# Attention layer: the softmax shift as transposed split columns, and an accumulator copy and its first use in another order

## The chip, the cores and the metric

The kernel runs on one core of one Trainium2 chip. The metric is the device time of one execution in microseconds (us). A change of more than 0.2% in either direction counts as a difference here; less counts as none.

## What is computed

Two layers over an image batch of 4 x 64 x 64 positions with 256 channels. Layer 0 (a state-space and convolution block) is untouched. Layer 1 is self-attention over the 4096 positions of each image, cut here to what matters:

```
f = xf @ Wf + bf            # keys,    32 channels
g = xf @ Wg + bg            # queries, 32 channels
hh = xf @ Wh + bh           # values, 256 channels
scores = einsum("bnd,bmd->bnm", g, f)
attn = softmax(scores, axis=-1)
o = einsum("bnm,bmc->bnc", attn, hh) @ Wo + bo
out = gamma * o + xf
```

The softmax needs a shift for each query: the maximum of its scores over all 4096 keys, taken off before the exponential.

## The kernel before

Layer 0 takes the first 2.6 ms and leaves keys, queries, values (each value as a high and a low part) and the residual in DRAM. `layer1` then works through 32 chunks of 512 queries (8 chunks for each of 4 images). A chunk `c` has 32 steps `m`, one for each 128 keys. Each engine runs its own instruction stream with explicit semaphores; the order is written out by hand in the function `body` of each engine, and nothing reorders it. The functions named below are on the lines of the profile.

In a step TensorE issues:

- `scores` (L1392), one pass into `ps_s`, for step m+2: it runs two steps ahead (`AHEAD`), so the scores of the next chunk's steps 0 and 1 are made in steps 30 and 31. The softmax shift is folded into this matmul: rows 96 and 97 of the query tile `gq` hold the negated maximum as a high and a low part, and the key tile `f_st` holds 1.0 in these rows.
- `scores_max` (L1375), one or two passes into `ps_m`, in steps 0 to 25: the scores of the next chunk against all keys, only for their maximum.
- `values_high` (L1401), four passes into `ps_o[0]` and `ps_o[1]`: the high part of the probabilities, times both parts of the values; `values_low` (L1409), two passes for the step before: the low part.
- in step 28 `spread_max` (L1382), which brings the maxima of the next chunk from one per partition to one per column.
- in steps 2, 4 and 6 the end of the chunk before: `sum_keys` (L1416) and `turn_half` (L1430, transposes of the accumulator copy `o_ch`).

ScalarE writes `ph` (L1502) and `probs` (L1504) from the scores, and in step 2 (`take_sums`) copies the old `ps_o[0]` into `o_ch` (L1488) and the old key sums `ps_a` into `sums` (L1492). VectorE reduces each `ps_m` to a maximum (`reduce_max`, L1514), adds the probabilities up in `ps_a` (L1543), copies the old `ps_o[1]` at the head of a chunk (`take_o`, L1548), and makes the shift in `finish_max`: the row maximum (L1519) in step 26, four diagonal 128 x 128 tiles `diag` (L1523) in step 27, and in step 29 two passes over the spread result (L1528 and L1532) that write rows 96 to 127 of `gq`. GpSimd makes `pl`, the low part of the probabilities (L1296). The queue of SyncE loads the queries of chunk c+2 (L1319) once the last `scores` of chunk c has run; at the last chunks of an image it also loads keys and values for the next image.

The first `values_high` of a chunk overwrites `ps_o`, so it waits on `o_out`, which the two copies into `o_ch` raise. The first `scores` of a chunk waits on `max_ok` for the finished `gq`.

Of the kernel before, what the change touches and what calls it, by code (L numbers as in the profile page):

```python
# [19 lines left out]
P = 128  # L20
# [1156 lines left out]
for _r in range(KEYS):  # L1177
    MAX_AT.setdefault(_r * MAX_STEPS // KEYS, []).append(_r)
MAX_REDUCE, MAX_DIAGONAL, MAX_SPREAD, MAX_ROWS = MAX_STEPS, MAX_STEPS + 1, MAX_STEPS + 2, MAX_STEPS + 3
AHEAD = 2  # L1180
# [6 lines left out]
def layer1(nc, keep, f_d, g_d, v_d, xres_d, out):  # L1187
# [5 lines left out]
    with ctx:  # L1193
# [18 lines left out]
        part_max = sb("part_max", [P, QT, PER_IMAGE])  # L1212
        row_max = sb("row_max", [P, QT])
        diag = sb("diag", [P, QT, P])
        max_hi = sb("max_hi", [P, TOK], F32R)
        pick = sb("pick", [P, 1])
        res = sb("res", [P, 2, QT, C])
# [61 lines left out]
        def _(pool):  # L1279

            for i, (part, value) in enumerate((
                    (f_st[96:P, :, :].bitcast(F32), 0.0), (pick[96:P, :], -1.0), (f_st[96:98, :, :].bitcast(F32), 1.0),
                    (pick[96:97, :], 0.0))):
                if i:
                    pool.wait_ge(const_ok, i)
                nc.gpsimd.memset(part, value).then_inc(const_ok, 1)

# [76 lines left out]
        def _(pe):  # L1364
# [13 lines left out]
            def spread_max(c):  # L1378

                pe.wait_ge(max_ok, 4 * c + 2)  # L1380
                for qt in range(QT):
                    mm = pe.matmul(ps_m[0][:, qt * P:(qt + 1) * P], ones[:, :], diag[:, qt, :], start=True, stop=True)  # L1382
                mm.then_inc(bcast_ok, 1)
# [55 lines left out]
            def body(c, par, img, half, at):  # L1439
                for m in range(KEYS):  # L1440
                    ending = m == KEYS - 1
                    values_high(c, m, 0)
                    if at != "first":
# [5 lines left out]
                    if at != "last":  # L1449
                        for r in MAX_AT.get(m, []):  # L1450
                            scores_max(c + 1, 1 - par, half + par, r, img + 1 if at == "turn" else None)
                        if m == MAX_SPREAD:
                            spread_max(c + 1)
                    if not ending:
                        values_high(c, m, 1)
# [14 lines left out]
            spread_max(0)  # L1470
            pe.wait_ge(const_ok, 4)
            for m in range(AHEAD):
# [6 lines left out]
        def _(act):  # L1479
# [3 lines left out]

            def take_sums(c):

                act.wait_ge(lo_done[0], KEYS * c + KEYS + DEPTH)
                act.wait_ge(turn_full, 2 * c + 2)
                nc.scalar.activation(o_ch[:, 0, :], ps_o[0][:, :], ACT.Copy).then_inc(o_out[0], 1)  # L1488
                act.wait_ge(acc_ok, KEYS * c + KEYS + DEPTH)
                if not (exact(c) and c == 0):  # L1490
                    act.wait_ge(sum_full, c)
                nc.scalar.activation(sums[:, :], ps_a[:, :], ACT.Copy).then_inc(sums_out, 1)  # L1492

            def body(c, par, img, half, at):
                for m in range(KEYS):
                    n = KEYS * c + m
                    if m == AHEAD and at != "first":
                        take_sums(c - 1)
# [6 lines left out]

            chunks(act, body)
            take_sums(B * PER_IMAGE - 1)

        @block.vector
        def _(dve):  # L1510
# [4 lines left out]

            def finish_max(c, what, par):
                if what == 0:
                    dve.wait_ge(max_out, KEYS * (c + 1) + 2)
                    nc.vector.tensor_reduce(row_max[:, :], part_max[:, :, :], AX.X, ALU.max).then_inc(max_ok, 1)  # L1519
                elif what == 1:  # L1520
                    dve.wait_ge(max_ok, 4 * c + 1)
                    for qt in range(QT):
                        last = nc.vector.tensor_scalar(diag[:, qt, :], ident[:, :], row_max[:, qt:qt + 1], -1.0,  # L1523
                                                       ALU.mult, ALU.mult)
                    last.then_inc(max_ok, 1)
                elif what == 2:
                    dve.wait_ge(bcast_ok, c + 1)
                    nc.vector.tensor_copy(max_hi[96:P, :], ps_m[0][96:P, :]).then_inc(max_ok, 1)  # L1528
                else:

                    dve.wait_ge(max_ok, 4 * c + 3)
                    nc.vector.scalar_tensor_tensor(gq[par][96:P, :], max_hi[96:P, :].bitcast(F32), pick[96:P, :],  # L1532
                                                   ps_m[0][96:P, :], ALU.mult, ALU.add).then_inc(max_ok, 1)

# [39 lines left out]
            def body(c, par, img, half, at):  # L1574
                if at != "first":
                    take_o(c - 1)
                for m in range(KEYS):
# [6 lines left out]
                    if at != "last":  # L1584
                        if m == MAX_REDUCE:
                            finish_max(c + 1, 0, 1 - par)
                        if m == MAX_DIAGONAL:
                            finish_max(c + 1, 1, 1 - par)
                        if m == MAX_ROWS:
                            finish_max(c + 1, 2, 1 - par)  # L1590
                            finish_max(c + 1, 3, 1 - par)

# [4 lines left out]
            for r in range(KEYS):  # L1597
                reduce_max(0, r)
            dve.wait_ge(const_ok, 4)
            for what in range(4):  # L1600
                finish_max(0, what, 0)
            chunks(dve, body)
# [49 lines left out]
```

## Time and profile before

| | |
|---|---|
| three runs | 4682.78, 4687.89 and 4689.73 us; median 4687.89 |
| profiled execution, first to last instruction (span) | 4687.7 us; no other time is recorded for it |
| its distance to the median of the runs | 0.2 us, under 0.01% |
| TensorE busy | 94% of the span |
| VectorE, ScalarE, GpSimd busy | 83%, 71%, 78% of the span |

The span is the time from the first to the last instruction of one profiled execution. A share of busy time is a mean over both layers. Layer 1 begins at about 2617 us. The start of a matmul in a timeline is what counts for its pace: its end is modelled and overlaps the next one, so two matmuls of 0.39 us can start 0.23 us apart.

### The profile page before, as it was taken

How to read it: one execution, taken by the hardware profiler on the slowest of the kernel's cores; microseconds unless marked ns; L12 is line 12 of the kernel's file. 1: busy time of each engine (PE TensorE's matmuls, PEld its weight loads, DVE VectorE, ACT ScalarE, POOL GpSimd, SP SyncE). 2: the span in 40 equal slices, each digit the busy share in tenths (PEclk: the TensorE clock that was granted, in tenths of full speed). 3: DMA queues.
4: the chain of work that ended last, by engine and by line, in shares of the span. 5: the costliest groups of instructions: out<-in, count | busy, mean ns of one | idle time of the engine just before them, and what ended most of it. 6: DMA issues, size and time to landing. Idle time of an engine off the chain costs nothing. (4 is left out here: it accounts for less than half of the span.)

```text
span 4687.7 us, 79434 instructions
## 1 busy us (share of the span) xinstructions
PE 4400.2 (94%) x24320; PEld 3132.5 (67%) x24320; DVE 3877.6 (83%) x7295; ACT 3348.9 (71%) x5828; POOL 3672.9 (78%) x3476
## 2 busy tenths in 40 slices
PE   5899999999999999999998899999999999999998
PEld 3556565656565656565655578878878777878887
DVE  4899999899989998999998577777777777777775
ACT  5888889888889888988896355555555555555555
POOL 4898989898989898989897366667666676666666
PEclk7899999999999999999999799999999999999999
DMA  2011111111111111111101400040001300040000
GB/s 82 21 40 47 36 48 35 48 35 47 36 46 37 48 35 47 36 49 34 49 29 43 128 22 17 17 120 21 22 22 45 90 22 20 22 121 22 15 19 19
DMA packets 139380, 198.15 MB, mean 42 GB/s; under 512 B 18458, under 2 KB 106500, under 8 KB 138756
## 3 DMA queue, kind: packets, MB, share of 16 engines
q1 hardware_dynamic: 139012, 193.76, 13.0%
q8 instruction: 168, 2.75, 0.2%
q14 instruction: 200, 1.64, 0.1%
HBM read 114.02 MB, written 79.69 MB: 41 GB/s over the span
## 5 line engine op out<-in xcount | busy, mean ns | idle before, releaser
L1296 POOL TENSOR_TENSOR pl<-probs,ph 128x512 fp32r<-128x512 f32 x1024 | 1322.1, 1292 | 641.9 <-PE ps_o L1409 324.3
L748 POOL TENSOR_TENSOR dec<-dt,rates 128x384 f32<-128x384 f32 x1536 | 1512.6, 1015 | 250.4 <-ACT dt L634 194.7
L1502 ACT ACTIVATE ph<-ps_s 128x512 fp32r<-128x512 f32 x1024 | 613.4, 599 | 897.7 <-PE ps_s L1392 891.9
L1514 DVE TENSOR_REDUCE part_max<-ps_m 128x1 f32<-128x512 f32 x1024 | 689.5, 689 | 386.1 <-PE ps_m L1375 385.6
L1401 PE MATMUL ps_o<-ph,vh 128*128 128x512 f32 x2048 | 812.3, 397 | 19.8 <-ACT o_ch L1488 19.6
L1401 PE MATMUL ps_o<-ph,vl 128*128 128x512 f32 x2048 | 805.5, 393 | 0.0
L1543 DVE TENSOR_TENSOR ps_a<-probs,ps_a 128x512 f32<-128x512 f32 x992 | 681.5, 687 | 40.9 <-ACT probs L1504 35.4
L1409 PE MATMUL ps_o<-pl,vh 128*128 128x512 f32 x2048 | 634.9, 391 | 0.0
L1504 ACT ACTIVATE probs<-ps_s 128x512 f32<-128x512 f32 x1024 | 608.2, 594 | 0.0
L906 DVE SCALAR_TENSOR_TENSOR psS<-u,bc,psS 128x384 f32<-128x384 f32 x1024 | 599.2, 614 | 1.2
L915 DVE SCALAR_TENSOR_TENSOR y_tok<-psS,bc,y_tok 128x384 f32<-128x384 f32 x960 | 553.8, 607 | 4.5
L763 POOL TENSOR_TENSOR y_tok<-y_tok,dec 128x384 f32<-128x384 f32 x512 | 512.8, 1001 | 18.1 <-DVE dec L896 14.2
L1401 PEld LDWEIGHTS ps_o<-ph,vh 128*128 128x128 f32 x2048 | 386.5, 189 | 116.4 <-ACT o_ch L1488 28.5
L442 PE MATMUL psF<-xnt,in_w 128*128 128x320 f32 (+1 forms) x1152 | 439.5, 511 | 23.2 <-ACT xp L613 12.3
L700 ACT ACTIVATE psS<-dec 128x384 f32<-128x384 f32 x512 | 255.2, 498 | 279.4 <-POOL dec L748 272.1
L892 DVE SCALAR_TENSOR_TENSOR psS<-u,bc,psS 128x384 f32<-128x384 f32 x512 | 314.1, 613 | 167.6 <-ACT psS L700 163.8
L1409 PEld LDWEIGHTS ps_o<-pl,vh 128*128 128x128 f32 x2048 | 384.6, 188 | 90.4
L1401 PEld LDWEIGHTS ps_o<-ph,vl 128*128 128x128 f32 x2048 | 387.7, 189 | 82.0
L701 ACT ACTIVATE dec<-dec 128x768 f32<-128x768 f32 x512 | 428.5, 837 | 0.0
L1392 PE MATMUL ps_s<-gq,f_st 128*128 128x512 f32 x1024 | 408.0, 399 | 1.6 <-issue 1.6
L1375 PE MATMUL ps_m<-f_max,gq 96*128 96x512 f32 x1024 | 387.0, 408 | 13.4 <-DMA f_max<-keys_d 9.1
L442 PEld LDWEIGHTS psF<-xnt,in_w 128*128 128x128 f32 x1152 | 218.8, 199 | 186.9 <-issue 114.9
(166 smaller groups left out, 7668.4 us busy)
## 6 DMA issues: line engine op xcount, KB each, us to landing
values_d<-hid SPq DMA_DIRECT2D x64, 512.0 KB, 4.1
xf<-in_x_dram SPq DMA_DIRECT2D x128, 128.0 KB
xb<-in_x_dram SPq DMA_DIRECT2D x128, 128.0 KB
residual_d<-xb SPq DMA_DIRECT2D x32, 512.0 KB, 2.7
vh<-values_d SPq DMA_DIRECT2D x32, 512.0 KB, 6.7
vl<-values_d SPq DMA_DIRECT2D x32, 512.0 KB, 7.7
res<-residual_d SPq DMA_DIRECT2D x32, 512.0 KB, 3.3
out_dram<-res SPq DMA_DIRECT2D x128, 128.0 KB
```

Source lines behind the costliest of these rows:

```text
L442: mm = pe.matmul(outs, wts[:, kb, :], src[:, kb], start=kb == 0, stop=kb == KB - 1)
L748: last = nc.gpsimd.tensor_tensor(dec[:, q % RING, j - 1, :], dt[:, par, d, token_of(d, j), :], rates[:, d, n, :], ALU.mult)
L763: nc.gpsimd.tensor_tensor(y_tok[:, par, t, :], y_tok[:, par, t, :], dec[:, q % RING, T - 2, :], ALU.add).then_inc(acc_ok, 1)
L906: nc.vector.scalar_tensor_tensor(s_t, u[:, d, t, :], scalar(q, t, "b"), s_t, ALU.mult, ALU.add).then_inc(state_ok, 1)
L915: nc.vector.scalar_tensor_tensor(y_t, s_t, scalar(q, t, "c"), y_t, ALU.mult, ALU.add).then_inc(state_ok, 1)
L1296: nc.gpsimd.tensor_tensor(pl[:, m % DEPTH, :], probs[:, m % DEPTH, :], ph[:, m % DEPTH, :].bitcast(F32), ALU.subtract).then_inc(pl_ok, 1)
L1401: mm = pe.matmul(ps_o[cb][:, :], v[:, m, cb * P:(cb + 1) * P], ph[:, m % DEPTH, :], start=m == 0 and v is vh, stop=False)
L1409: pe.matmul(ps_o[cb][:, :], vh[:, m, cb * P:(cb + 1) * P], pl[:, m % DEPTH, :], start=False, stop=m == KEYS - 1).then_inc(lo_done[cb], 1)
L1502: nc.scalar.activation(ph[:, m % DEPTH, :], ps_s[m % 2][:, :], ACT.Exp).then_inc(ph_ok, 1)
L1504: nc.scalar.activation(probs[:, m % DEPTH, :], ps_s[m % 2][:, :], ACT.Exp).then_inc(probs_ok, 1)
L1514: nc.vector.tensor_reduce(part_max[:, qt, kc:kc + 1], ps_m[r % 2][:, :], AX.X, ALU.max).then_inc(max_out, 1)
L1543: nc.vector.tensor_tensor(ps_a[:, :], probs[:, m % DEPTH, :], ps_a[:, :], ALU.add).then_inc(acc_ok, 1)
```

## The change

The four 128 x 128 diagonals are gone. A block `shift_hl` of four 128 x 128 tiles is set to zero once; for each chunk VectorE writes only columns 96 and 97 of each tile, with the high and the low part of the negated maximum (`shift_parts`: a reduction with a negated result into four columns of `ps_t`, a rounding copy, a subtraction). `spread_max` transposes the four tiles, so that rows 96 and 97 of `ps_m` come out as the two parts and the other rows as zeros. One copy (`shift_rows`) puts rows 96 to 127 into `gq`, now in step 28.

ScalarE's copy of `ps_o[0]` moves from step 2 to step 1 (`take_o`), ahead of the exponentials of step 1; the copy of the key sums stays in step 2. TensorE's first `values_high` of a chunk moves behind the `scores` and `scores_max` of step 0. In the diff, cut to its core, the functions of TensorE come first, then those of ScalarE, then those of VectorE.

```
-MAX_REDUCE, MAX_DIAGONAL, MAX_SPREAD, MAX_ROWS = MAX_STEPS, MAX_STEPS + 1, MAX_STEPS + 2, MAX_STEPS + 3
+MAX_REDUCE, MAX_SPREAD, MAX_ROWS = MAX_STEPS, MAX_STEPS + 2, MAX_STEPS + 2
...
+            nc.gpsimd.memset(shift_hl[:, :, :], 0.0).then_inc(const_ok, 1)
...
             def spread_max(c):
-                pe.wait_ge(max_ok, 4 * c + 2)
+                pe.wait_ge(max_ok, 4 * c + 3)
                 for qt in range(QT):
-                    mm = pe.matmul(ps_m[0][:, qt * P:(qt + 1) * P], ones[:, :], diag[:, qt, :], start=True, stop=True)
+                    mm = pe.transpose(ps_m[0][:, qt * P:(qt + 1) * P], shift_hl[:, qt, :], ident[:, :])
                 mm.then_inc(bcast_ok, 1)
...
             def body(c, par, img, half, at):
                 for m in range(KEYS):
                     ending = m == KEYS - 1
-                    values_high(c, m, 0)
+                    if m > 0:
+                        values_high(c, m, 0)
...
                         if m == MAX_SPREAD:
                             spread_max(c + 1)
+                    if m == 0:
+                        values_high(c, m, 0)
                     if not ending:
                         values_high(c, m, 1)
...
-            def take_sums(c):
+            def take_o(c):
                 act.wait_ge(lo_done[0], KEYS * c + KEYS + DEPTH)
                 act.wait_ge(turn_full, 2 * c + 2)
                 nc.scalar.activation(o_ch[:, 0, :], ps_o[0][:, :], ACT.Copy).then_inc(o_out[0], 1)
+
+            def take_sums(c):
                 act.wait_ge(acc_ok, KEYS * c + KEYS + DEPTH)
...
+                    if m == 1 and at != "first":
+                        take_o(c - 1)
                     if m == AHEAD and at != "first":
                         take_sums(c - 1)
...
-            def finish_max(c, what, par):
-                if what == 0:
-                    dve.wait_ge(max_out, KEYS * (c + 1) + 2)
-                    nc.vector.tensor_reduce(row_max[:, :], part_max[:, :, :], AX.X, ALU.max).then_inc(max_ok, 1)
-                elif what == 1:
-                    dve.wait_ge(max_ok, 4 * c + 1)
-                    for qt in range(QT):
-                        last = nc.vector.tensor_scalar(diag[:, qt, :], ident[:, :], row_max[:, qt:qt + 1], -1.0,
-                                                       ALU.mult, ALU.mult)
-                    last.then_inc(max_ok, 1)
-                elif what == 2:
-                    dve.wait_ge(bcast_ok, c + 1)
-                    nc.vector.tensor_copy(max_hi[96:P, :], ps_m[0][96:P, :]).then_inc(max_ok, 1)
-                else:
-                    dve.wait_ge(max_ok, 4 * c + 3)
-                    nc.vector.scalar_tensor_tensor(gq[par][96:P, :], max_hi[96:P, :].bitcast(F32), pick[96:P, :],
-                                                   ps_m[0][96:P, :], ALU.mult, ALU.add).then_inc(max_ok, 1)
+            def shift_parts(c):
+                row, hi, lo = ps_t[:, 0:QT], shift_hl[:, :, 96], shift_hl[:, :, 97]
+                dve.wait_ge(max_out, KEYS * (c + 1) + 2)
+                if not (exact(c) and c == 0):
+                    dve.wait_ge(turn_out, QT * (c - 1) + QT)
+                    dve.wait_ge(bcast_ok, c)
+                nc.vector.tensor_reduce(row, part_max[:, :, :], AX.X, ALU.max, negate=True).then_inc(max_ok, 1)
+                dve.wait_ge(max_ok, 4 * c + 1)
+                nc.vector.tensor_copy(hi.bitcast(F32R), row).then_inc(max_ok, 1)
+                dve.wait_ge(max_ok, 4 * c + 2)
+                nc.vector.tensor_tensor(lo.bitcast(F32R), row, hi, ALU.subtract).then_inc(max_ok, 1)
+
+            def shift_rows(c, par):
+                dve.wait_ge(bcast_ok, c + 1)
+                nc.vector.tensor_copy(gq[par][96:P, :], ps_m[0][96:P, :]).then_inc(max_ok, 1)
```

The names behind the operations in the rows below are what is written and, after the arrow, what is read; in brackets stand the semaphores that the instruction waits for. TensorE before, from the last `values_low` of a chunk to the second `values_high` of the next:

```order
L1409 MATMUL ps_o<-pl,vh 128x512 x2
L1401 MATMUL ps_o<-ph,vh 128x512 [waits o_out0,ph_ok]
L1401 MATMUL ps_o<-ph,vl 128x512
L1392 MATMUL ps_s<-gq,f_st 128x512 [waits probs_ok]
L1375 MATMUL ps_m<-f_max,gq 128x512 [waits max_out,g_loaded0]
L1375 MATMUL ps_m<-f_max,gq 128x512 [waits max_out]
L1401 MATMUL ps_o<-ph,vh 128x512 [waits o_out1]
```

TensorE now, at the same place:

```order
L1405 MATMUL ps_o<-pl,vh 128x512 x2
L1388 MATMUL ps_s<-gq,f_st 128x512 [waits probs_ok]
L1371 MATMUL ps_m<-f_max,gq 128x512 [waits max_out,g_loaded0]
L1371 MATMUL ps_m<-f_max,gq 128x512 [waits max_out]
L1397 MATMUL ps_o<-ph,vh 128x512 [waits o_out0,ph_ok]
L1397 MATMUL ps_o<-ph,vl 128x512
L1397 MATMUL ps_o<-ph,vh 128x512 [waits o_out1]
```

The two passes that wait for `o_out0` stood first in the chunk and now stand behind one `scores` and two `scores_max` passes; the wait for the loaded queries (`g_loaded0`) has moved ahead of them.

ScalarE at the same chunk start, before (steps 1 and 2 of the new chunk):

```order
L1502 ACTIVATE ph<-ps_s 128x512 [waits pl_ok,hi_done,s_full]
L1504 ACTIVATE probs<-ps_s 128x512 [waits acc_ok]
L1486 REGISTER_ALU
L1487 ISA [waits lo_done0]
L1488 ACTIVATE o_ch<-ps_o 128x512 [waits turn_full]
L1492 ACTIVATE sums<-ps_a 128x512 [waits sum_full,acc_ok]
L1499 REGISTER_ALU
L1502 ACTIVATE ph<-ps_s 128x512 [waits pl_ok,hi_done,s_full]
L1504 ACTIVATE probs<-ps_s 128x512 [waits acc_ok]
```

ScalarE now (from the exponentials of step 0 on):

```order
L1506 ACTIVATE ph<-ps_s 128x512 [waits pl_ok,hi_done,s_full]
L1508 ACTIVATE probs<-ps_s 128x512 [waits acc_ok]
L1485 REGISTER_ALU
L1486 ISA [waits lo_done0]
L1487 ACTIVATE o_ch<-ps_o 128x512 [waits turn_full]
L1503 REGISTER_ALU
L1506 ACTIVATE ph<-ps_s 128x512 [waits pl_ok,hi_done,s_full]
L1508 ACTIVATE probs<-ps_s 128x512 [waits acc_ok]
L1494 ACTIVATE sums<-ps_a 128x512 [waits sum_full,acc_ok]
L1503 REGISTER_ALU
```

The copy into `o_ch` has moved ahead of one `ph` and one `probs`; the copy into `sums` stands where it stood.

VectorE in steps 26 to 30, before:

```order
L1543 TENSOR_TENSOR ps_a<-probs,ps_a 128x512 [waits acc_ok,probs_ok] x2
L1519 TENSOR_REDUCE row_max<-part_max 128x4 [waits max_out]
L1543 TENSOR_TENSOR ps_a<-probs,ps_a 128x512 [waits acc_ok,probs_ok]
L1523 TENSOR_SCALAR diag<-ident,row_max 128x128 [waits max_ok]
L1523 TENSOR_SCALAR diag<-ident,row_max 128x128 x3
L1543 TENSOR_TENSOR ps_a<-probs,ps_a 128x512 [waits acc_ok,probs_ok] x2
L1528 CAST max_hi<-ps_m 32x512 [waits bcast_ok]
L1532 SCALAR_TENSOR_TENSOR gq<-max_hi,pick,ps_m 32x512 [waits max_ok]
L1543 TENSOR_TENSOR ps_a<-probs,ps_a 128x512 [waits acc_ok,probs_ok] x2
```

VectorE now, at the same place:

```order
L1547 TENSOR_TENSOR ps_a<-probs,ps_a 128x512 [waits acc_ok,probs_ok] x2
L1528 TENSOR_REDUCE ps_t<-part_max 128x4 [waits bcast_ok,turn_out,max_out]
L1530 CAST shift_hl<-ps_t 128x4 [waits max_ok]
L1532 TENSOR_TENSOR shift_hl<-ps_t,shift_hl 128x4 [waits max_ok]
L1547 TENSOR_TENSOR ps_a<-probs,ps_a 128x512 [waits acc_ok,probs_ok] x2
L1537 CAST gq<-ps_m 32x512 [waits bcast_ok]
L1547 TENSOR_TENSOR ps_a<-probs,ps_a 128x512 [waits acc_ok,probs_ok] x3
```

All three small instructions of the shift stand in step 26, and the one copy that writes `gq` stands one step earlier than the two instructions before.

## Rows read from the trace of the kernel before

**Rows 1.** The page, its first line

```profile
span 4687.7 us, 79434 instructions
```

**Rows 2.** Stretches: us, busy (instructions) by engine, PEclk, DMA share, GB/s

```profile
2700.00:4680.00 1980.00, 1934.85 (x8725) 1576.56 (x8724) 1479.95 (x2405) 1117.43 (x2062) 1372.04 (x1124) 1.00 0.12 37
...
3672.00:3676.00 4.00, 4.00 (x13) 3.15 (x12) 2.09 (x4) 1.52 (x3) 1.51 (x2) 0.66 0.09 30
3676.00:3680.00 4.00, 4.00 (x23) 3.42 (x23) 2.53 (x6) 1.75 (x4) 1.81 (x2) 1.00 0.00 0
```

**Rows 3.** TensorE's waits, 2700 to 4680 us: total, times, longest

```profile
PE ps_o L1401 <- ACT o_ch L1488: 19.6, 31, 6.0
PE ps_m L1382 <- DVE diag L1523: 19.1, 18, 1.1
PE ps_m L1375 <- DMA gq<-queries_d: 3.1, 2, 1.9
```

**Rows 4.** Timeline of TensorE, a spread without a wait: start, us, instruction

```profile
3468.48 0.39 PE L1392 MATMUL ps_s<-gq,f_st 128*128 128x512 f32 x1
3468.75 1.16 PE L1382 MATMUL ps_m<-diag,ones 128*128 128x128 f32 x8
3469.66 0.48 PE L1401 MATMUL ps_o<-ph,vh 128*128 128x512 f32 x1
3469.98 0.40 PE L1401 MATMUL ps_o<-ph,vl 128*128 128x512 f32 x1
```

**Rows 5.** Timeline of TensorE, a spread with a wait, its idle time in brackets

```profile
3405.53 1.16 PE L1382 MATMUL ps_m<-diag,ones 128*128 128x128 f32 x8 [1.06 <-DVE diag L1523]
```

**Rows 6.** Timeline of VectorE before that spread; durations of all diagonals

```profile
3401.73 0.18 DVE L1519 TENSOR_REDUCE row_max<-part_max 128x4 f32<-128x32 f32 x1
...
3402.53 2.94 DVE L1523 TENSOR_SCALAR diag<-ident,row_max 128x128 f32<-128x128 f32 x4
...
L1523 DVE TENSOR_SCALAR diag<-ident,row_max x128: 273/279/1347, 2647.1 to 4612.7; 128x128 f32<-128x128 f32 x128
```

**Rows 7.** Timeline of TensorE, four transposes and the pass behind them

```profile
3422.70 0.60 PE L1430 MATMUL ps_t<-ident,o_ch 128*128 128x128 f32 x4
3423.05 0.48 PE L1392 MATMUL ps_s<-gq,f_st 128*128 128x512 f32 x1
```

**Rows 8.** Timeline of TensorE at a chunk start

```profile
3475.46 0.61 PE L1409 MATMUL ps_o<-pl,vh 128*128 128x512 f32 x2
3476.38 0.50 PE L1401 MATMUL ps_o<-ph,vh 128*128 128x512 f32 x1 [0.31 <-ACT o_ch L1488]
3476.72 0.39 PE L1401 MATMUL ps_o<-ph,vl 128*128 128x512 f32 x1
3476.95 0.39 PE L1392 MATMUL ps_s<-gq,f_st 128*128 128x512 f32 x1
```

**Rows 9.** Timelines of ScalarE and VectorE at that chunk start

```profile
3475.24 0.59 ACT L1504 ACTIVATE probs<-ps_s 128x512 f32<-128x512 f32 x1
3475.72 0.61 ACT L1488 ACTIVATE o_ch<-ps_o 128x512 f32<-128x512 f32 x1
...
3476.21 0.69 DVE L1548 COPY o_ch<-ps_o 128x512 f32<-128x512 f32 x1 [2.73 <-PE ps_o L1409]
```

**Rows 10.** The load of the queries: its queue, all landings, the longest waits

```profile
3471.82 0.33 SPq L1319 DMA_DIRECT2D gq<-queries_d  x1
...
DMA to landing us min/median/max: 2.3/2.5/6.9
...
3161.41 0.72 PE L1375 MATMUL ps_m<-f_max,gq 96*128 96x512 f32 x2 [1.20 <-DMA gq<-queries_d]
```

**Rows 11.** Timeline of ScalarE at the start of chunk 16

```profile
3670.83 0.60 ACT L1488 ACTIVATE o_ch<-ps_o 128x512 f32<-128x512 f32 x1 [4.26 <-issue]
```

**Rows 12.** Timeline of VectorE ahead of the first chunk

```profile
2650.19 0.70 DVE L1528 CAST max_hi<-ps_m 32x512 fp32r<-32x512 f32 x1 [2.17 <-PE ps_m L1382]
2650.92 0.76 DVE L1532 SCALAR_TENSOR_TENSOR gq<-max_hi,pick,ps_m 32x512 fp32r<-32x512 f32 x1
```

More of the change, by code:

```diff
@@ L1212, in layer1 @@
         part_max = sb("part_max", [P, QT, PER_IMAGE])
[L1213 to L1216, printed above, removed]
+        shift_hl = sb("shift_hl", [P, QT, P])
         res = sb("res", [P, 2, QT, C])
@@ L1279, in _ @@
         def _(pool):
[L1281 to L1286, printed above, removed]
+            nc.gpsimd.memset(f_st[96:P, :, :].bitcast(F32), 0.0).then_inc(const_ok, 1)
+            pool.wait_ge(const_ok, 1)
+            nc.gpsimd.memset(shift_hl[:, :, :], 0.0).then_inc(const_ok, 1)
+            pool.wait_ge(const_ok, 2)
+            nc.gpsimd.memset(f_st[96:98, :, :].bitcast(F32), 1.0).then_inc(const_ok, 1)
             pool.sem_inc(pl_ok, DEPTH)
@@ L1470, in _ @@
             spread_max(0)
-            pe.wait_ge(const_ok, 4)
+            pe.wait_ge(const_ok, 3)
             for m in range(AHEAD):
@@ L1506, in _ @@
             chunks(act, body)
+            take_o(B * PER_IMAGE - 1)
             take_sums(B * PER_IMAGE - 1)
@@ L1585, in body @@
                         if m == MAX_REDUCE:
-                            finish_max(c + 1, 0, 1 - par)
-                        if m == MAX_DIAGONAL:
-                            finish_max(c + 1, 1, 1 - par)
+                            shift_parts(c + 1)
                         if m == MAX_ROWS:
-                            finish_max(c + 1, 2, 1 - par)
-                            finish_max(c + 1, 3, 1 - par)
+                            shift_rows(c + 1, 1 - par)
             dve.sem_inc(max_out, 2)
@@ L1598, in _ @@
                 reduce_max(0, r)
-            dve.wait_ge(const_ok, 4)
-            for what in range(4):
-                finish_max(0, what, 0)
+            dve.wait_ge(const_ok, 3)
+            shift_parts(0)
+            shift_rows(0, 0)
             chunks(dve, body)
```

## The prediction

> **What bounds the kernel now.** I read the stretches first. From 2700 to 4680 us TensorE is busy for 1934.85 of 1980 us at a granted clock of 1.00, the next engine (VectorE) for 1480, ScalarE and GpSimd for less [rows 2]. So layer 1 is bound by TensorE's stream, and time can come from two sources only: passes taken out of it, and gaps closed in it. The list of TensorE's waits names the gaps: 19.6 us at 31 chunk starts, behind ScalarE's copy into `o_ch`, and 19.1 us at 18 of 31 spreads, behind the diagonals; then 3.1 us for queries that have not landed [rows 3]. The change touches the first two and the passes of the spread. The timelines say what a gap really costs, since idle time alone is less than the loss.
>
> A pass of 512 columns takes a slot of 0.23 us (3476.72 to 3476.95, rows 8); I use that below.
>
> **The spread's wait.** Unhindered, the spread starts 0.27 us after the `scores` pass before it (3468.48 to 3468.75), which overlaps that pass's 0.39 us by 0.12 [rows 4]. In the other kind it starts with 1.06 us idle, so 1.18 us later than it could [rows 5]. Why: on VectorE the row maximum (0.18 us) is at 3401.73, but the four diagonals begin a step later and take 2.94 us together, since a single one ranges from 273 to 1347 ns [rows 6]. Now three small instructions follow each other from 3401.73. The reduction costs 0.18. A 128x4 copy and a subtraction are in no row; from below 0.18 each (the reduction's), from above 1.35 each (the longest diagonal, one that was held up). I take 0.2, as they read the row from PSUM like the other PSUM readers of VectorE, and a gap of 0.05 each: ready by 3402.4, and by 3404.7 at the worst. TensorE comes free for the spread at 3404.47 (3405.53 less 1.06). So the wait goes, or 0.2 to 0.3 us of it stay. The gain is 18 x 1.18 = **21.2 us**; at the upper bound some 7 less.
>
> **The spread itself.** Four products with ones run as 8 passes and hold TensorE from 3468.75 to 3469.66, 0.91 us [rows 4]. Four transposes of the same shape run as 4 passes and hold it from 3422.70 to 3423.05, 0.35 us; the pass behind them starts in the same way, with 0.48 us [rows 7]. That is 0.56 us for each of 31 spreads, **17.4 us**. VectorE's copy and its second pass become one, 0.76 us less, and stand one step earlier; what waits for them, the first `scores` of the next chunk, is 13 slots (3.0 us) behind the spread, and the copy takes 0.70 [rows 12]. VectorE may wait there for the spread with one or two additions queued behind; it is idle for a quarter of the stretch [rows 2]. I cost this at nothing.
>
> **The chunk start.** The last two `values_low` start at 3475.46 and a slot later, so TensorE is free at 3475.92; the first `values_high` starts at 3476.38 (0.31 us of it counted as idle), and its follower comes 0.34 us later, not 0.23 [rows 8]. A stop thus costs 0.46 + 0.11 = 0.57 us, its idle time plus 0.26. Over 31 starts: 19.6 + 31 x 0.26 = 27.7 us.
>
> What would remain? ScalarE's copy starts at 3475.72, back to back behind `probs` of step 1 [rows 9]. VectorE's copy of the other half starts 0.52 us after its last `values_low` (3475.69 to 3476.21); the last `values_low` of ScalarE's half is four slots older, so by the same 0.52 us its copy could start at 3475.30. TensorE is released 0.66 us after the copy's start (3475.72 to 3476.38), so at 3475.96. Meanwhile it has three other passes (the moved `scores` and two `scores_max`) until 3476.61. Margin 0.65 us: the wait goes, including the longer ones (up to 1.2 us) of starts where ScalarE is late. The exponentials of step 1 slip by one copy, some 0.5 us, to about 3476.9, and are wanted at about 3477.5. The tightest is VectorE's half, untouched: released at 3476.21 + 0.69 + 0.05 = 3476.95, wanted at 3476.61 + 0.46 = 3477.07.
>
> Three starts are different. At chunks 8 and 24 the queries' load sets the time of the first `scores_max` (3161.41, rows 10; two waits, 3.1 us, rows 3). It lands when it did, so the 0.57 us are not gained, and two `values_high` that used to run under the wait now stand behind it: 2 x (0.57 + 0.46) = 2.1 us off. At chunk 16 the longest wait (6.05 us) is ScalarE's own, 4.26 us for nothing that the profile shows [rows 11]; nothing here removes that. Of its 6.3 us I count the three passes that now run under it, 0.7 us, so 5.6 us off. The sum is 27.7 - 2.1 - 5.6 = **20.0 us**.
>
> **Ahead of the first chunk** the second pass over the spread result goes (0.76 us), half of the 8 passes for which the copy waited 2.17 us (1.0), and of the four diagonals (0.27 us each at the least, rows 6) against two small instructions at most 0.6, which I take as 0.3 [rows 12]: **2.1 us**. The additional memset of GpSimd lies under the 32 maxima of this stretch.
>
> **Sum.** 21.2 + 17.4 + 20.0 + 2.1 = 60.7 us. Against the profiled span of 4687.7 [rows 1], which is 0.2 us from the median of the runs, that gives **4627 us**, 1.3% less.
>
> **Rivals.**
>
> *The chunk start gets a new wait* (chance 0.15). The margin of VectorE's half is 0.12 us, and a weight load wants its semaphore earlier than the matmul. If each of 28 starts keeps a stop for it, that costs the restart of 0.11 to the whole 0.57: 3 to 16 us, so 4630 to 4643. For it: 0.12 us is thin. Against it: a wait's first pass starts with the release, not after a load (3476.38, rows 8).
>
> *The shift is still late* (0.05). VectorE's small writes into SBUF are held up as the diagonals are. Worked out above: 0.2 to 0.3 us at 31 spreads, 7 to 9 us, 4636; were the whole wait kept, 4648. For it: the row with 1347 ns. Against it: 2.7 us of room.
>
> *Slower, through the queries' load* (0.02). `scores_max` waits for it, and it now stands ahead of the first values of every chunk with nothing left to cover it. Issued at 3471.82 and landed 2.5 us later by the median, it is there by 3474.3; wanted at 3475.92 + 0.23 = 3476.15. Both move together when stops ahead of the issue go, so 1.8 us of room. Lateness beyond that costs 31 times its size: the gain of 60.7 us is used up at 1.96 us, so from landings of 6.3 us on in all chunks. At 7 us it would be 31 x 2.7 - 61 = 22 us slower, 4710. The longest landing is 6.9 us, but only at the turn of an image; the median speaks against it [rows 10].
>
> *The clock* (0.02). Around the stop at chunk 16 the granted clock fell to half (1.2 GHz of 2.4), and a stretch of 4 us at 0.66 held 13 passes where the next at 1.00 held 23 [rows 2]. If four transposes in place of products let the clock fall once a chunk, that is 10 slots, 2.3 us, 31 times: 71 us, more than the gain, 4698. Against it: each chunk has 8 transposes and 8 one-column products already, and the mean is 1.00 over 1980 us.
> The Trainium skill (TensorE: Matmul & The Clock Gate, Part 4: PE-mode transpose) says that a transpose does not count as TensorE being busy in the way that lifts the clock; by it this change would feed the gate less. The trace does not bear it out: the clock stays at 1.00 through the transposes of `turn_half`.
> On the port that VectorE and GpSimd share, the Trainium skill (SBUF — State Buffer, SBUF: two separate sides) says that a VectorE instruction in a two-port mode blocks against GpSimd as a whole, one that reads PSUM and at most one SBUF tensor does not. By it the old diagonals are held and the new copy and subtraction are not; the sum by the rule is the one above, the sum by the longest diagonal 7 us less.
>
> **How the numbers follow.** The forecast as worked out has 0.72, with a range of its own of 4618 to 4637: below, because each stop may cost more than I read and chunk 16 may lose less of its clock (13 passes against 23 is up to 2 us), above by the small losses. The rival of the chunk start has 0.15, the late shift 0.05, the two others 0.02 each, and 0.04 is for what I have not seen. To hold 8 in 10 the range takes the likeliest and most of the first rival: 4618 to 4642. 0.2% of this time is 9.4 us, about what a measurement can tell from no change. Faster by more than that: 0.95; within it: 0.01; slower: 0.04.
>
> **What would show it.** In the changed trace: no wait of TensorE behind the subtraction; 4 passes for the spread in 0.35 us, 128 in all; no wait behind `o_ch` except at chunk 16; copy and subtraction at about 0.2 us. The forecast is wrong if waits of similar length appear at the head of the chunk behind VectorE's `o_ch`, `probs` or the queries, if the small writes take 0.8 us or more, or if the clock of the stretch falls below 1.00.

## The result and the profile after

The changed kernel takes 4635.19 us (median of 4 runs, 4627.51 to 4638.9) against 4688.81 us before: ratio 0.9883, 95% interval 0.9869 to 0.9897, so 1.2% faster. The forecast was 4627 us, with a range of 4618 to 4642. In a second set of runs it took 4629.64 us (0.9877). The profiled run took 4627.51 us and has a span of 4625.6 us.

The page's first line and the list of TensorE's waits from 2700 to 4622 us (total, times, longest) answer to [rows 1, 3]:

```profile
span 4625.6 us, 79138 instructions
...
PE ps_m L1371 <- DMA gq<-queries_d: 5.6, 2, 3.1
PE ps_s L1388 <- issue: 4.8, 1, 4.8
PE ps_t L1426 <- DVE res L1569: 1.0, 1, 1.0
PE ps_t L1426 <- DVE total L1560: 0.6, 1, 0.6
PE ps_t L1412 <- ACT sums L1494: 0.3, 1, 0.3
```

The 18 waits behind the diagonals and the 31 behind `o_ch` are gone. What is left stands at three places: the loads at chunks 8 and 24, and one stop at chunk 16; the last three rows, 1.9 us in all, are the end of the last chunk and were there before (0.27, 0.63 and 0.97 us). The stretches answer to [rows 2]; the third and the fourth hold the stops of chunks 8 and 16:

```profile
2700.00:4620.00 1920.00, 1903.99 (x8567) 1560.09 (x8565) 1386.48 (x2300) 1108.14 (x2052) 1365.13 (x1119) 1.00 0.13 38
...
3000.00:3100.00 100.00, 100.00 (x456) 82.27 (x456) 73.61 (x125) 58.77 (x110) 71.82 (x60) 1.00 0.15 39
3134.00:3144.00 10.00, 6.87 (x23) 5.17 (x23) 3.70 (x6) 4.13 (x8) 3.69 (x4) 0.83 0.63 198
3629.00:3640.00 11.00, 6.20 (x18) 4.67 (x17) 2.58 (x4) 4.42 (x9) 3.82 (x3) 0.72 0.68 211
```

In an ordinary stretch TensorE now shows no idle time at all. Its timeline at a spread and at the chunk start behind it, against [rows 4, 5, 8]:

```profile
3439.64 0.39 PE L1388 MATMUL ps_s<-gq,f_st 128*128 128x512 f32 x1
3439.86 0.60 PE L1378 MATMUL ps_m<-ident,shift_hl 128*128 128x128 f32 x4
3440.22 0.48 PE L1397 MATMUL ps_o<-ph,vh 128*128 128x512 f32 x1
...
3446.02 0.62 PE L1405 MATMUL ps_o<-pl,vh 128*128 128x512 f32 x2
3446.47 0.39 PE L1388 MATMUL ps_s<-gq,f_st 128*128 128x512 f32 x1
3446.70 0.63 PE L1371 MATMUL ps_m<-f_max,gq 96*128 96x512 f32 x2
3447.17 0.39 PE L1397 MATMUL ps_o<-ph,vh 128*128 128x512 f32 x1
3447.40 0.40 PE L1397 MATMUL ps_o<-ph,vl 128*128 128x512 f32 x1
3447.64 0.40 PE L1397 MATMUL ps_o<-ph,vh 128*128 128x512 f32 x1
```

The spread starts one slot behind `scores` and holds TensorE for 0.36 us in place of 0.91. At the chunk start every pass follows its predecessor after 0.23 us: no stop, no slow restart. ScalarE's copy starts 0.52 us after the start of the `values_low` pass that it waits for (the second of the pair at 3445.11, so 3445.34), as worked out; on VectorE the three small instructions cost 0.18, 0.17 and 0.16 us:

```profile
3445.86 0.60 ACT L1487 ACTIVATE o_ch<-ps_o 128x512 f32<-128x512 f32 x1 [1.04 <-PE ps_o L1405]
```

```profile
3437.21 0.18 DVE L1528 TENSOR_REDUCE ps_t<-part_max 128x4 f32<-128x32 f32 x1
3437.43 0.17 DVE L1530 CAST shift_hl<-ps_t 128x4 fp32r<-128x4 f32 x1
3437.64 0.16 DVE L1532 TENSOR_TENSOR shift_hl<-ps_t,shift_hl 128x4 fp32r<-128x4 f32 x1
```

Not all of the 62.1 us between the two spans belongs to the change. Layer 0 is the same code, yet the first `scores_max`, with which layer 1 begins on TensorE, stands 6.7 us earlier. From the source views of that line, before and after:

```profile
L1375 PE MATMUL ps_m<-f_max,gq x1024: 387/395/797, 2619.8 to 4607.8; 96*128 96x512 f32 x171
```

```profile
L1371 PE MATMUL ps_m<-f_max,gq x1024: 389/395/796, 2613.1 to 4546.9; 96*128 96x512 f32 x171
```

From there to the end it is 2067.9 us before (4687.7 - 2619.8) and 2012.5 after: **55.4 us** come from layer 1. In the profiles of the experiments that first start lies between 2612.0 and 2619.1 us, without any relation to the edit, so a span by itself is uncertain by some 8 us here.

### The profile page after: what moved, and what is told of

The parts are those of the page before. It is cut to its first block and busy times, and to the rows that moved or that the text cites. A ratio compares the mean times of both kernels' runs of the same rounds, so it can differ in the third digit from the quotient of the medians.

```text
span 4625.6 us, 79138 instructions
## 1 busy us (share of the span) xinstructions
PE 4367.7 (94%) x24192; PEld 3118.8 (67%) x24192; DVE 3788.5 (82%) x7199; ACT 3345.0 (72%) x5828; POOL 3673.9 (79%) x3475
## 3 DMA queue, kind: packets, MB, share of 16 engines
q1 hardware_dynamic: 139012, 193.76, 13.2%
```

## The experiments

All ratios are to the kernel before on the same chip. Three sets ran, each on a chip of its own: `after_again`, `shift_only`, `order_only` and `no_pe_move`; then `no_act_move`, `diagonal_early`, `row_in_sbuf` and `queries_first`; then `psum_step27`, `sbuf_step27`, `queries_first_2` and `values_late`. The 95% interval of a ratio is about 0.0014 wide on each side, which is some 7 us, so a difference of two medians is no finer than that. The length of layer 1 in a profile, from the first `scores_max` to the end, is free of what layer 0 does and is given beside it; it is one profile each, and the two of the changed kernel differ by 2.6 us.

**The changed kernel again** (`after_again`).

> The changed kernel once more, beside the others on one chip. Both theories expect about 0.988 of the kernel before. If the 7 to 11 us between its fastest and slowest runs come from layer 0, which the change does not touch, layer 1 has the same length here as in the first profile (2002.8 us from its first to its last matmul) while the span differs.

4629.64 us, 0.9877 (0.9862 to 0.9892). Span 4631.8, layer 1 from 2616.7, so 2015.1 us for layer 1 against 2012.5 in the first profile. Layer 0 shows 3.6 us of the difference of 6.2, layer 1 the rest, at the loads: 6.6 us of waits for queries in place of 5.6, and a half clock behind both. So my expectation, that layer 1 has always the same length, was wrong in part: its image turns vary too.

**The shift alone** (`shift_only`): the moves on TensorE and ScalarE undone.

```
-                    if m > 0:
-                        values_high(c, m, 0)
+                    values_high(c, m, 0)
...
-                    if m == 0:
-                        values_high(c, m, 0)
...
-                    if m == 1 and at != "first":
-                        take_o(c - 1)
                     if m == AHEAD and at != "first":
+                        take_o(c - 1)
                         take_sums(c - 1)
```

> The split, the transposes and the single copy, with the accumulator copy and the first values pass where they stood before. If the parts add up (my theory), the spread's wait (21.2 us), its passes (17.4) and 2.1 ahead of the first chunk come out: 40.7 us less than before, and TensorE still waits some 19.6 us at 31 chunk starts. Rival: what the spread gives back is partly taken again at the chunk start, because ScalarE is then later against TensorE; then the waits at the chunk start grow beyond 25 us and the gain is under 33 us.

4646.08 us, 0.9909 (0.9894 to 0.9924): 41.5 us less than before (4687.55), forecast 40.7. Its waits:

```profile
PE ps_o L1397 <- ACT o_ch L1484: 18.2, 31, 5.2
PE ps_m L1371 <- DMA gq<-queries_d: 4.6, 2, 2.6
```

The waits at the chunk start are no longer than they were (18.2 us against 19.6, rows 3), so the spread's gain is not taken again there. The rival falls.

**The order alone** (`order_only`): the same moves made in the kernel before.

> The two moves at the chunk start alone, with the diagonals and the products with ones. If the parts add up, 20 us less than before, the 31 waits behind the accumulator copy are gone and 18 waits behind the diagonals stay at 1.06 us. Rival: a TensorE that runs ahead meets the diagonals in every chunk, so that the 13 spreads without a wait get one of 1 us too; then the gain is some 5 us.

4667.34 us, 0.9962 (0.9948 to 0.9976): 20.2 us less, forecast 20.

```profile
PE ps_m L1382 <- DVE diag L1532: 19.0, 18, 1.1
PE ps_m L1375 <- DMA gq<-queries_d: 5.4, 2, 2.9
PE ps_s L1392 <- ACT probs L1512: 4.8, 1, 4.8
```

Still 18 waits behind the diagonals and not 31, so this rival falls too. 41.5 + 20.2 = 61.7 us against 57.9 for both together on that chip: the parts add up within the intervals. By the length of layer 1 the shift alone gives 37.0 us (2067.9 - 2030.9) and the order alone 17.5 (2067.9 - 2050.4), together 54.5 against 55.4 and 52.8 in the two profiles with both. So the parts add up, and that both medians came within 1 us of their forecasts is in part luck.

**TensorE's move undone** (`no_pe_move`): the first two hunks of the diff above alone.

> The changed kernel with the first values pass back at the head of the chunk; ScalarE's copy stays moved. By the prediction's times the copy releases TensorE at 0.04 us after it comes free, so a stop costs only 0.04 plus the restart of 0.11: under 5 us over 31 starts, and at the two image turns two passes run under the wait for the queries again (0.9 us back). So 0 to 4 us slower than the changed kernel. Rival: the move on TensorE carries the gain, and without it some 15 us come back.

4629.65 us, 0.9878 (0.9863 to 0.9894): no difference to the changed kernel. One wait of 0.2 us behind `o_ch` is left, beside the large one of chunk 16. An ordinary chunk takes 61.3 us from spread to spread in place of 61.2.

**ScalarE's move undone** (`no_act_move`): its last hunk alone.

> The changed kernel with ScalarE's copy back behind the exponentials of step 1; TensorE's move stays. In an ordinary chunk the copy releases TensorE 0.46 us after it comes free, and three moved passes take 0.69, so no wait is left there; only the five starts where ScalarE is late (0.9 us more) keep some 0.7 us each. So 2 to 5 us slower than the changed kernel. Rival: ScalarE's move carries the gain, and without it some 15 us come back.

4633.23 us, 0.9885 (0.987 to 0.99).

```profile
PE ps_m L1371 <- DMA gq<-queries_d: 5.1, 2, 2.6
PE ps_s L1388 <- issue: 4.8, 1, 4.8
PE ps_o L1397 <- ACT o_ch L1487: 1.9, 5, 0.6
```

Five waits, as expected, at the starts where ScalarE is late; the time cannot be told from the changed kernel's. So either move alone opens the chunk start: ScalarE's copy comes early enough, or TensorE has three other passes to run until it comes. They are not two gains of 10 us but one gain of 20, bought twice.

**The diagonals one step earlier** (`diagonal_early`): one number in the kernel before.

```
-MAX_REDUCE, MAX_DIAGONAL, MAX_SPREAD, MAX_ROWS = MAX_STEPS, MAX_STEPS + 1, MAX_STEPS + 2, MAX_STEPS + 3
+MAX_REDUCE, MAX_DIAGONAL, MAX_SPREAD, MAX_ROWS = MAX_STEPS, MAX_STEPS, MAX_STEPS + 2, MAX_STEPS + 3
```

> The kernel before with one number changed: the four diagonals stand in step 26, right behind the row maximum, not in step 27. If the spread waits because the diagonals begin late (my reading), they end 0.7 us sooner, and the 18 waits of 1.06 us shrink to about 0.4 or vanish: 10 to 20 us less than before. If it waits because they are long (held up by GpSimd for most of 2.94 us, wherever they stand), they stay as long or become longer, and the gain is under 5 us.

4662.19 us, 0.9943 (0.993 to 0.9957): 24.0 us less than before, more than either theory gave. By the length of layer 1 it is 23.0 us (2067.9 - 2044.9). TensorE does not wait for the diagonals at all from chunk 1 on. To see why, take first GpSimd of the kernel before, beside the diagonals that began at 3402.53 and took 2.94 us [rows 6]:

```profile
3402.50 1.29 POOL L1296 TENSOR_TENSOR pl<-probs,ph 128x512 fp32r<-128x512 f32 x1 [0.55 <-ACT probs L1504]
3404.09 1.30 POOL L1296 TENSOR_TENSOR pl<-probs,ph 128x512 fp32r<-128x512 f32 x1 [0.29 <-ACT probs L1504]
```

The first diagonal began just behind a `pl` and ended with it, the last met the next one. VectorE and GpSimd at the same chunk of the new kernel:

```profile
3391.34 0.18 DVE L1519 TENSOR_REDUCE row_max<-part_max 128x4 f32<-128x32 f32 x1
3391.56 1.93 DVE L1523 TENSOR_SCALAR diag<-ident,row_max 128x128 f32<-128x128 f32 x4
```

```profile
3390.27 1.29 POOL L1296 TENSOR_TENSOR pl<-probs,ph 128x512 fp32r<-128x512 f32 x1 [0.55 <-PE ps_o L1409]
3392.11 1.29 POOL L1296 TENSOR_TENSOR pl<-probs,ph 128x512 fp32r<-128x512 f32 x1 [0.55 <-ACT probs L1504]
```

Three of the four now fall into the 0.55 us in which GpSimd is idle, and only the fourth is held (1.34 us, from 3392.15 on). The traces know two kinds of chunk. In the 18 whose spread waited, the diagonals took 2.94 us before and take 1.93 now; in the 13 others they took 1.92, which was short enough, and take 0.88 now:

```profile
3329.10 0.18 DVE L1519 TENSOR_REDUCE row_max<-part_max 128x4 f32<-128x32 f32 x1
3329.31 0.88 DVE L1523 TENSOR_SCALAR diag<-ident,row_max 128x128 f32<-128x128 f32 x4
```

```profile
3328.10 1.29 POOL L1296 TENSOR_TENSOR pl<-probs,ph 128x512 fp32r<-128x512 f32 x1 [0.55 <-PE ps_o L1409]
3329.94 1.40 POOL L1296 TENSOR_TENSOR pl<-probs,ph 128x512 fp32r<-128x512 f32 x1 [0.55 <-ACT probs L1504]
```

So in the 18 chunks the diagonals begin 0.6 us sooner behind the row maximum (0.22 us after its start in place of 0.80) and are 1.0 us shorter; the two together exceed the 1.18 us that the spread lost, and neither does alone. Each of my theories had one half: the diagonals were late, and they were long because of what ran beside them, not wherever they stand.

**The row of maxima in SBUF** (`row_in_sbuf`).

```
+        row_sb = sb("row_sb", [P, QT])
...
-                row, hi, lo = ps_t[:, 0:QT], shift_hl[:, :, 96], shift_hl[:, :, 97]
+                row, hi, lo = row_sb[:, :], shift_hl[:, :, 96], shift_hl[:, :, 97]
```

> The changed kernel with the row of maxima in SBUF in place of PSUM, so that the rounding copy reads and writes SBUF and the subtraction reads two SBUF operands. If the small writes owe their speed to the PSUM source, the copy and the subtraction take 0.5 to 1.35 us in many chunks, as the diagonals did; the time stays the same within 2 us, since 2.7 us of room lie ahead of the spread. Rival: small instructions are not held up at all, and both stay near 0.2 us.

4626.1 us, 0.9872 (0.9857 to 0.9887), no difference. The copy takes 170 to 173 ns and the subtraction 166 to 169 in all 32 chunks: not held up, against my expectation. In step 26 they too fall into GpSimd's gap. So the pair was repeated where the diagonals had stood.

**The small instructions in step 27, from PSUM and from SBUF** (`psum_step27`, `sbuf_step27`): the changed kernel and `row_in_sbuf`, each with

```
-MAX_REDUCE, MAX_SPREAD, MAX_ROWS = MAX_STEPS, MAX_STEPS + 2, MAX_STEPS + 2
+MAX_REDUCE, MAX_SPREAD, MAX_ROWS = MAX_STEPS + 1, MAX_STEPS + 2, MAX_STEPS + 2
```

> The changed kernel with the three small instructions of the shift in step 27, the place where the diagonals stood, at which GpSimd's pl runs beside them. Theory: an instruction that reads PSUM and at most one SBUF tensor is never held up by GpSimd; then copy and subtraction stay at 0.17 us, the shift is ready 1 us ahead of the spread and the time equals the changed kernel within 2 us. Rival: whatever writes SBUF there is held up; then one of them takes up to 1.3 us and TensorE waits up to 1 us at the spread.

> The same, with the row of maxima in SBUF. Theory: the copy (SBUF to SBUF) and the subtraction (two SBUF operands) are held up for the rest of a running pl instruction, as the diagonals were: 0.5 to 1.3 us in place of 0.17, and TensorE waits 0 to 1 us at the spreads, 0 to 25 us in all. Rival: instructions of 4 columns are too short to be held up, and both stay at 0.17 us as they did in step 26; then the size of the diagonals, not their operands, made them collide.

Copy and subtraction of the first (durations in ns: least, median, longest), then of the second:

```profile
L1530 DVE CAST shift_hl<-ps_t x32: 164/165/166, 2645.2 to 4555.3; 128x4 fp32r<-128x4 f32 x32
L1532 DVE TENSOR_TENSOR shift_hl<-ps_t,shift_hl x32: 164/166/167, 2645.4 to 4555.5; 128x4 fp32r<-128x4 f32 x32
```

```profile
L1531 DVE CAST shift_hl<-row_sb x32: 170/1075/1216, 2638.8 to 4548.8; 128x4 fp32r<-128x4 f32 x32
L1533 DVE TENSOR_TENSOR shift_hl<-row_sb,shift_hl x32: 166/167/169, 2639.0 to 4549.9; 128x4 fp32r<-128x4 f32 x32
```

This settles it for the copy. In 31 of the 32 chunks it runs beside GpSimd's `pl` in both kernels (the first one, ahead of the chunks, has no `pl`). There a copy of 4 columns from SBUF to SBUF takes 1073 to 1216 ns, 1075 by the median, and the same copy from PSUM 165 ns. The subtraction of the second stays short though it reads two SBUF operands: it follows when the copy has waited `pl` out, so no run here says what it would do beside GpSimd. Both kernels are as fast as the changed one (4631.64 us, 0.9881, and 4630.07 us, 0.9883), since even 1.2 us fit into the room ahead of the spread. The Trainium skill (SBUF — State Buffer, section SBUF: two separate sides) says that a VectorE instruction in a two-port mode and a GpSimd instruction exclude each other for the whole instruction; the traces agree with it, with 0.28 us for a diagonal by itself against 1.34 behind a `pl` that had just begun, and 165 against 1075 ns here. That the diagonals and the copy run in such a mode is not seen in any trace.

**Queries first at the image turn** (`queries_first`): aimed at what the changed kernel still waits for.

```
-                for j in range(PER_IMAGE - 1 if at == "turn" else 0):
+                for j in range(PER_IMAGE - 2 if at == "turn" else 0):
...
                 if at not in ("late", "last"):
                     sp.wait_ge(s_full, KEYS * c + KEYS)
                     load_queries(c + 2, par)
                 if at == "turn":
                     sp.wait_ge(lo_done[1], KEYS * (c + 1) + DEPTH)
-                    load_keys_values(img + 1, PER_IMAGE - 1)
+                    for j in range(PER_IMAGE - 2, PER_IMAGE):
+                        load_keys_values(img + 1, j)
```

> The changed kernel, where at the last chunk of an image the queries are loaded ahead of the last two blocks of keys and values, not between them. If the waits at chunks 8 and 24 (3.1 and 2.5 us of TensorE) come from the queue of 1.2 MB ahead of the queries, the queries land in about 2.5 us, both waits go and the clock does not fall at chunk 8: 6 to 9 us less than the changed kernel. Rival: the landing is late because all 16 DMA engines are busy whatever stands in front; then under 2 us.

4617.21 us, 0.9851 (0.9836 to 0.9866). From the first `scores_max` at 2613.6 us to the end of the span of 4615.8 it is 2002.2 us, 10.3 less than in the first profile of the changed kernel and 12.9 less than in the second. Its only wait of TensorE from 2700 to 4600 us:

```profile
PE ps_s L1389 <- ACT probs L1509: 2.4, 1, 2.4
```

Both waits for the queries are gone; the longest landing is 5.3 us in place of 7.5, though not the 2.5 that I had written. The gain is above the 6 to 9 us expected, because the stop at chunk 16 halved as well (4.8 to 2.4 us). From spread to spread, chunk 8 takes 61.2 us in place of 66.2, chunk 24 61.2 in place of 63.8 and chunk 16 66.8 in place of 68.8.

**The same again, and with the last loads later** (`queries_first_2`, `values_late`): in the second, the line that waits reads `KEYS * (c + 1) + 8 + DEPTH`.

> The kernel with the queries ahead of the last two blocks of keys and values once more, as the neighbour of the next one: 0.985 of the kernel before.

> The same, with the last two blocks of keys and values of an image turn loaded eight steps later, inside the next chunk. If the wait at chunk 16 (2.4 us of TensorE with the queries first, 4.8 before that, with a drop of the clock behind it) comes from these loads standing ahead of the code that the engines fetch when the outer loop jumps back, chunk 16 falls from 66.8 to some 62 us: 3 to 5 us less. Rival: the fetch takes its time whatever the DMA engines do, and chunk 16 stays at 66 to 67 us.

4616.63 us, 0.985 (0.9835 to 0.9865), and 4615.27 us, 0.9847 (0.9834 to 0.9861). The wait at chunk 16 is 2.1 us in the first and 2.7 in the second:

```profile
PE ps_s L1389 <- ACT probs L1509: 2.7, 1, 2.7
```

From spread to spread chunk 16 takes 63.6 us in the first and 64.2 in the second. Neither 62 nor 66 to 67 us came, but the neighbour decides: the same kernel had 66.8 us there in its first profile, because 14 passes behind the stop stood 0.43 us apart, and in these two profiles the passes stand 0.23 us apart almost at once. So a chunk 16 of some 64 us is no gain of the later loads. Moving them out of the way does nothing more, so they are not what the rest of that stop comes from. The stop occurs only where the outer loop jumps back; ScalarE, VectorE and GpSimd all wait there for nothing that the profile shows (4.3, 4.0 and 3.5 us in the changed kernel). That they wait for their code is an argument, not something these runs show.

## Why the prediction was right, step by step

- *The spread's wait, 21.2 us.* All 18 waits went. The kernel with the early diagonals isolates them: 24.0 us less by the medians (20 to 33 us by the interval of the ratio), 23.0 by the length of layer 1. Right in its size. The reason was incomplete: I had named the late start and "a single one that was held up", and had not looked at GpSimd's timeline beside it.
- *The spread itself, 17.4 us.* 0.91 became 0.36 us (3439.86 to 3440.22) at 31 spreads, 17.1 us. Right by the timelines. The difference of `shift_only` and `diagonal_early`, which would isolate it, is 17.5 us by the medians and 14.0 by the length of layer 1 (2044.9 - 2030.9), so it confirms no more than the size.
- *The chunk start, 20.0 us.* `order_only` gave 20.2 by the medians and 17.5 by the length of layer 1. The mechanism was right, and more robust than I had it: either move is enough. In the changed kernel an ordinary chunk without a wait at its spread is 1.06 to 1.13 us shorter, forecast 0.56 + 0.57, and one with it, where ScalarE's copy was on time, 2.27 to 2.44, forecast 2.31. The thin margin of 0.12 us of VectorE's half held; no wait of TensorE behind it is in the list.
- *Ahead of the first chunk, 2.1 us.* The finished `gq` comes 31.9 us after the first `scores_max` before (2650.92 + 0.76 - 2619.8) and 29.3 us after it now (by the row below, 2641.74 + 0.70 - 2613.1): 2.5 us. But not all of it is kept: in the first step of chunk 0 TensorE now has no values passes ahead of the `scores` pass, and waits there (second row).

```profile
2641.74 0.70 DVE L1537 CAST gq<-ps_m 32x512 fp32r<-32x512 f32 x1 [1.21 <-PE ps_m L1378]
2644.48 0.79 PE L1388 MATMUL ps_s<-gq,f_st 128*128 128x512 f32 x1 [0.75 <-ACT probs L1508]
```

- *The image turns* are the term that was mis-sized most. I had taken the landing of the queries as fixed and charged 2.1 us for chunks 8 and 24, in which TensorE's own clock had no part. In the changed kernel the wait at chunk 8 is 3.13 us, not 1.20 [rows 10], and the clock falls behind it:

```profile
3138.70 1.06 PE L1371 MATMUL ps_m<-f_max,gq 96*128 96x512 f32 x2 [3.13 <-DMA gq<-queries_d]
3139.56 0.63 PE L1397 MATMUL ps_o<-ph,vh 128*128 128x512 f32 x1
3139.99 0.63 PE L1397 MATMUL ps_o<-ph,vl 128*128 128x512 f32 x1
```

  Passes stand 0.43 us apart, at 1.2 GHz instead of 2.4, for 8 of them: some 1.6 us more. The wait itself is 0.9 us longer than 1.20 plus the 1.03 that I had added: the waiting pass starts 6.95 us after its load is issued (3131.75), before it was 6.05 (3155.36). Together 2.5 us at chunk 8 in this profile; in the second profile the clock fell behind a wait of 3.7 us at chunk 24 as well. That is half of the distance between 60.7 us forecast and 55.4 us found in layer 1.

- *The rest* shows when both profiles are cut at the starts of the spreads. The forecast of each part follows the prediction's own rules (0.56 us for a spread, idle time plus 0.12 for its wait, idle time plus 0.26 for a stop at a chunk start, and its corrections for chunks 8, 16 and 24). In the first row it is the 2.1 us from above and one wait of 1.18:

| from spread to spread | before, us | after, us | less by | forecast |
|---|---|---|---|---|
| first `scores_max` to the spread in chunk 0 | 89.4 | 87.1 | 2.3 | 3.3 |
| 27 ordinary chunks (1 to 30 without 8, 16, 24) | 1707.0 | 1652.8 | 54.1 | 54.7 |
| chunk 8 | 63.8 | 66.2 | -2.4 | 0.1 |
| chunk 16 | 69.5 | 68.8 | 0.7 | 1.3 |
| chunk 24 | 64.5 | 63.8 | 0.7 | 0.1 |
| last spread to the end | 73.6 | 73.7 | -0.1 | 1.2 |

  The ordinary chunks, where the change does its work, are right within 0.02 us each on average. The prediction named chunk 16 as a place that might lose less of its clock; it lost more, with 12 passes at half pace behind the stop against 7 before. In the last chunk 0.8 us are lost behind its last `sum_keys` (14.0 us to the end, before 13.2); that, and the other 0.5 us missing in its row, I cannot explain.
- *The rivals.* No new wait at the chunk start; the shift is never late; the clock is 1.00 in the stretches of ordinary chunks, with transposes in each, as the trace before had said. The Trainium skill's sentence on transposes (TensorE: Matmul & The Clock Gate, Part 4: PE-mode transpose) is hardly tested by this: the 12 transposes of a chunk hold TensorE for some 1.1 us of 61. The load of the queries did cost time, by the mechanism of that rival, but only at two chunks. `queries_first` measured what they are worth: of the some 12 us that it gained (4629.64 and 4617.21 us, on two chips) the two chunks have 7.6 against the first profile of the changed kernel and 10.3 against the second, and chunk 16 has 2.0 and 1.8.
- *The level.* The forecast stood on one profiled span. The median of the first runs is 8 us above it, that of the second set 3 us. The first start of layer 1 moves by 8 us between profiles of the same layer 0; a forecast of a level can't be better than that, while the ratio is little touched by it. That one came out at 0.9883 against 0.9870, and the 0.0013 between them is 6 us, about the distance found in layer 1.

## What to carry to other kernels

When an instruction of VectorE takes 0.28 us in one place and 1.3 in another, look at what GpSimd runs at that moment: moving it one step, or letting it read PSUM, can be worth as much as making it smaller (here 24 us of 4688 for one step). A wait at a hand-over can be closed from either side, by an earlier producer or by other work ahead of the consumer; try one before paying for both. When stops are taken out of a dense engine, ask which load lands near them: one that was 1.2 us late before was 3.1 us late after, and an idle time of two or three us can also cost the clock behind it.

## What the runs showed of the hardware that I had not expected

A copy of 128x4 elements from SBUF to SBUF took 1075 ns (median of 32) beside a GpSimd operation of 1.29 us, and 171 ns in its gap; from PSUM it took 165 ns in both places. It also works the other way: in the 13 chunks where the last early diagonal began some 0.03 us before a `pl`, the diagonal took 0.28 us and that `pl` 1.40 in place of 1.29; in the 18 where it began some 0.04 us behind one, the `pl` took 1.29 us and the diagonal 1.34.

Behind an idle time of 3.13 us TensorE's passes stood 0.43 us apart, and the granted clock was 0.83 over 10 us. In the same profile, behind the 2.42 us at chunk 24, they stood 0.23 us apart as ever, and so they did behind the 1.20 us of the kernel before [rows 10]. The length of the idle time alone does not decide it: behind 1.86 us at chunk 8 in `diagonal_early` 7 passes stood 0.43 us apart, from the sixth on, and behind 2.86 us at chunk 24 in `order_only` none did. At chunk 16 of one and the same kernel it was 14 passes behind 2.44 us (`queries_first`) and none behind 2.10 (`queries_first_2`), and the chunk took 66.8 us the one time and 63.6 the other.
